# A fused linear-attention and feed-forward kernel: the last tiles written out engine by engine in another order, dead buffers for x1 and y, and Wq and Wk issued by SyncE

## The reference

```python
q = exp(split_heads(x @ Wq.T + bq)); k = exp(split_heads(x @ Wk.T + bk)); v = split_heads(x @ Wv.T + bv)
num = einsum(q, cumsum(k[..., :, None] * v[..., None, :]))
den = sum(q * cumsum(k))
x1  = layernorm(x + merge_heads(num / den) @ Wo.T + bo)
out = layernorm(x1 + tanh(x1 @ weight @ aux_weight1 @ aux_weight2 + bias))
```

## Time and profile before

| | us |
|---|---|
| median of 3 runs | 2287.44 (2287.05 to 2289.54) |
| the profiled execution | 2287.53 |
| its span | 2285.8 |
| mean granted clock of TensorE | 0.996 |
| PE busy | 2239.1 (98%) |
| DVE busy | 1546.1 (68%) |
| POOL busy | 1250.8 (55%) |
| ACT busy | 1014.6 (44%) |

### The profile page before, as it was taken

The page is one execution under the profiler, slowest core; times in us unless marked ns, Lnnn a source line. Parts: engine busy times, 40 slices in busy tenths (PEclk is TensorE's granted clock), DMA queues, the critical chain, the costliest instruction groups (busy, mean ns, idle before and its releaser), DMA issues.

```text
span 2285.8 us, 77469 instructions
## 1 busy us (share of the span) xinstructions
PE 2239.1 (98%) x27848; PEld 1829.1 (80%) x27848; DVE 1546.1 (68%) x2456; ACT 1014.6 (44%) x1695; POOL 1250.8 (55%) x1797
## 2 busy tenths in 40 slices
PE   7999999999999999999999999999999999999996
PEld 5778888888888888888888888888888888878874
DVE  4566766776776776676676677677677667667675
ACT  4344444444444444444444444444444444444443
POOL 2355555555555555555555555555555555555554
PEclk9999999999999999999999999999999999999999
DMA  8233333333333333333333333333333333333221
GB/s 179 65 100 106 116 106 103 116 108 103 113 111 102 110 114 100 108 118 102 107 116 104 105 116 106 103 116 108 103 112 112 99 112 114 102 105 116 70 75 47
DMA packets 292414, 241.60 MB, mean 106 GB/s; under 512 B 33184, under 2 KB 224160, under 8 KB 292128
## 3 DMA queue, kind: packets, MB, share of 16 engines
q1 hardware_dynamic: 290976, 235.02, 33.2%
q10 hardware_dynamic: 1152, 2.10, 0.4%
HBM read 139.20 MB, written 97.78 MB: 104 GB/s over the span
## 4 chain that ended last, share of the span: by engine, by line
PE 95%; DVE 1%; issue 1%; ACT 1%; POOL 1%; DMA 1%; SPq 0%; POOLq 0%; ACTq 0%; DVEq 0%
PE SC L339 26%; PE SC L341 25%; PE SC L340 25%; PE SC L430 6%; PE ND L406 6%; PE ND L397 3%; PE ND L393 2%; PE ND L441 2%; DMA WK<-a 1%; DVE o L828 0%; SPq L261 0%; POOL oL L958 0%; ACT A L661 0%; PE ND L339 0%; PE ND L341 0%
## 5 line engine op out<-in xcount | busy, mean ns | idle before, releaser
L940 POOL TENSOR_SCALAR_AFFINE_SELECT A<-A 128x512 f32<-128x512 f32 x512 | 329.7, 676 | 384.2 <-ACT A L661 384.1
L835 DVE TENSOR_TENSOR WK<-SC,bfbc 128x512 f32<-128x512 f32 x128 | 88.6, 692 | 623.1 <-PE SC L341 623.1
L828 DVE RECIPROCAL o<-ND 128x512 f32<-128x512 f32 x128 | 427.7, 3342 | 6.3 <-POOL oL L958 6.3
L952 POOL TENSOR_TENSOR x1L<-WK,x1H 128x512 fp32r<-128x512 f32 x125 | 161.6, 1293 | 469.7 <-ACT x1H L674 469.7
L661 ACT ACTIVATE A<-SC 128x512 f32<-128x512 f32 x512 | 264.6, 603 | 101.9 <-PE SC L430 101.9
L674 ACT ACTIVATE x1H<-WK 128x512 fp32r<-128x512 f32 x125 | 79.1, 633 | 334.4 <-DVE WK L872 334.4
L688 ACT ACTIVATE WK<-xres,shift,rstd 128x512 f32<-128x512 f32 x128 | 104.3, 815 | 276.5 <-POOL shift L968 276.5
L841 DVE TENSOR_TENSOR_SCAN WK<-ones,k,KT 128x128 f32<-128x128 f32 x512 | 207.3, 468 | 14.8 <-PE ND L393 14.8
L339 PE MATMUL SC<-xTH,WqH 128*128 128x512 f32 x512 | 209.4, 409 | 1.0 <-ACT A L661 1.0
L629 ACT ACTIVATE QT<-SC,bcol 128x512 f32<-128x512 f32 x128 | 88.3, 690 | 269.5 <-PE SC L341 269.5
L339 PE MATMUL SC<-WfH,x1H 128*128 128x512 f32 x512 | 199.7, 390 | 7.4 <-ACT x1H L672 3.0
(11 more groups left out here) (110 smaller groups left out, 5008.1 us busy)
## 6 DMA issues: line engine op xcount, KB each, us to landing
xres<-x SPq DMA_DIRECT2D x128, 256.0 KB, 2.7
out<-WK SPq DMA_DIRECT2D x128, 256.0 KB, 3.1
xin<-x SPq DMA_DIRECT2D x504, 64.0 KB, 1.9
x_rows<-WK SPq DMA_DIRECT2D x125, 256.0 KB, 2.0
WK<-x_rows SPq DMA_DIRECT2D x500, 64.0 KB, 2.1
k_rows<-WK SPq DMA_DIRECT2D x120, 256.0 KB, 2.1
WK<-k_rows SPq DMA_DIRECT2D x480, 64.0 KB, 1.9
A<-a1T SPq DMA_DIRECT2D x4, 256.0 KB, 6.2
```

The costliest lines, as they stand in the source:

```text
L828: nc.vector.reciprocal(o[:, :, :], den_ps).then_inc(recip_ready, 1)
L835: nc.vector.tensor_tensor(yf, ffn_ps, bfbc[:, :], ALU.add).then_inc(z_ready, 1)
L940: last = nc.gpsimd.affine_select(out=A[:, k % 2, j, :, :], in_=A[:, k % 2, j, :, :], compare_op=ALU.is_ge, fill=0.0, base=0, pattern=[[0, ...
L952: nc.gpsimd.tensor_tensor(halves[1], x1s[:, :].rearrange("p (t g q) -> p g t q", t=HG, q=HD), halves[0].bitcast(F32), ALU.subtract).then_i ...
```

## The change: what it does

The loop of the kernel is not touched but for the same code being put into named helpers. Two things change.

At the end, run_slots stops earlier (PE after slot 126, DVE after 126, ACT and POOL after 127), and each engine gets an `end()` with its remaining stages in an order of its own. Tiles 126 and 127 (`at_end`) write x1 to WK 4 and 5 and y to WK 6 and 7, and tile 126 uses oH and oL for the halves of x1. The turns of x1 are taken out of `feed_forward`.

At the start, SP issues the loads of Wq and Wk behind tile 3 and ahead of the biases; ACT issues no DMA any more.

```diff
@@ helpers
+        def x1_of(c, n):
+            return WK[:, 4 + n % 2, :] if c.at_end(n) else x1[:, n % 2, :]
+        def y_of(c, n):
+            return WK[:, 6 + n % 2, :] if c.at_end(n) else y[:, n % 2, :]
+        def x1_halves(c, n):
+            return (oH, oL) if c.at_end(n) and not c.at_end(n - 1) else (x1H, x1L)
@@ SyncE
             load_x(first, 3)
+            load_blocks(sp, wq_raw, wqT, wq_loaded)
+            load_blocks(sp, wk_raw, wkT, wk_loaded)
             load_biases()
@@ TensorE
+            def turn_x1(c, n):
+                pe.wait_ge(identity_ready, 1)
+                pe.wait_ge(scores_out[1], NT)
+                wait(pe, x1h_ready, c.count(n))
+                wait(pe, x1l_ready, c.count(n))
+                wait(pe, x1_ready, c.count(n + 1))
...
+            def end():
+                first_half(*place(NT - 1))
+                output_projection(*place(NT - 3))
+                denominators(*place(NT - 1))
+                attend(*place(NT - 1))
+                output_projection(*place(NT - 2))
+                feed_forward(*place(NT - 4))
+                turn_x1(*place(NT - 3))
+                output_projection(*place(NT - 1))
+                turn_x1(*place(NT - 2))
+                feed_forward(*place(NT - 3))
+                turn_x1(*place(NT - 1))
+                feed_forward(*place(NT - 2))
+                feed_forward(*place(NT - 1))
@@ ScalarE
+            def write_x1(c, n):
+                wait(act, shift1_ready, c.count(n + 1))
+                if not c.at_end(n):
+                    wait(act, y_ready, c.count(n - 1))
...
+            def end():
+                split_o(*place(NT - 1))
+                tanh(*place(NT - 4))
+                split_turned_x1(*place(NT - 3))
+                write_x1(*place(NT - 2))
+                split_turned_x1(*place(NT - 2))
+                write_out(*place(NT - 4))
+                write_x1(*place(NT - 1))
+                split_turned_x1(*place(NT - 1))
+                tanh(*place(NT - 3))
+                write_out(*place(NT - 3))
+                tanh(*place(NT - 2))
+                tanh(*place(NT - 1))
+                write_out(*place(NT - 2))
+                write_out(*place(NT - 1))
             split_aux(0)
-            load_blocks(act, wq_raw, wqT, wq_loaded)
             split_aux(1)
-            load_blocks(act, wk_raw, wkT, wk_loaded)
@@ VectorE
+            def end():
+                sum_ffn(*place(NT - 5))
+                prefix_sums(*place(NT - 1))
+                normalise(*place(NT - 2))
+                add_bias(*place(NT - 3))
+                turn_x1(*place(NT - 4))
+                statistics(*place(NT - 5))
+                residual(*place(NT - 3))
+                add_bias(*place(NT - 2))
+                normalise(*place(NT - 1))
+                residual(*place(NT - 2))
+                sum_ffn(*place(NT - 4))
+                rest_of_turned_x1(*place(NT - 3))
+                add_bias(*place(NT - 1))
+                statistics(*place(NT - 4))
+                residual(*place(NT - 1))
+                rest_of_turned_x1(*place(NT - 2))
+                sum_ffn(*place(NT - 3))
+                rest_of_turned_x1(*place(NT - 1))
+                statistics(*place(NT - 3))
+                sum_ffn(*place(NT - 2))
+                sum_ffn(*place(NT - 1))
+                statistics(*place(NT - 2))
+                statistics(*place(NT - 1))
@@ GpSimd
+            def end():
+                rest_of_o(*place(NT - 1))
+                scale_x1(*place(NT - 2))
+                add_x1(*place(NT - 4))
+                scale_out(*place(NT - 4))
+                scale_x1(*place(NT - 1))
+                add_x1(*place(NT - 3))
+                scale_out(*place(NT - 3))
+                add_x1(*place(NT - 2))
+                add_x1(*place(NT - 1))
+                scale_out(*place(NT - 2))
+                scale_out(*place(NT - 1))
```

More of the change, by code:

```diff
@@ L575, in _ @@
             second_half(*place(NT - 2 * B))
-            for t in range(NT - 2 * B + 1, NT + 3):
+            for t in range(NT - 2 * B + 1, NT - 1):
                 first_half(*place(t))
                 second_half(*place(t))
+            end()
         @block.scalar
@@ new lines, in split_o @@
+            def split_o(c, n):
+                wait(act, o_ready, c.count(n + 1))
+                wait(act, oproj_done, c.count(n))
+                nc.scalar.activation(oH[:, :, :], o[:, :, :], ACT.Copy).then_inc(oh_ready, 1)
+            def write_x1(c, n):
+                wait(act, shift1_ready, c.count(n + 1))
+                if not c.at_end(n):
+                    wait(act, y_ready, c.count(n - 1))
+                nc.scalar.activation(x1_of(c, n), xres[:, n % 2, :], ACT.Identity, bias=shift[:, 0:1],
+                                     scale=rstd[:, 0:1]).then_inc(x1_ready, 1)
@@ L648, in slot, with tanh, write_out @@
+            def tanh(c, n):
+                wait(act, z_ready, c.count(n + 1))
+                nc.scalar.activation(y_of(c, n), y_of(c, n), ACT.Tanh).then_inc(tanh_ready, 1)
+            def write_out(c, n):
+                wait(act, shift2_ready, c.count(n + 1))
+                nc.scalar.activation(y_of(c, n), y_of(c, n), ACT.Identity, bias=shift[:, 1:2],
+                                     scale=rstd[:, 1:2]).then_inc(out_ready, 1)
             def slot(c, k):
-                att = c.exists(k)
@@ L650, in slot @@
                 proj = c.exists(k + 4)
[L651 to L662, removed]
+                if c.exists(k - 4):
+                    tanh(c, k - 4)
@@ L663, in slot @@
+                keep_scores(c, k)
                 if proj:
                     keep_q(c, k)
-                if att and not proj:
+                else:
                     copy_v(c, k)
                 if c.exists(k - 3):
[L668 to L676, removed]
@@ new lines, in normalise, with add_bias @@
+            def normalise(c, n):
+                wait(dve, num_done, c.count(n + 1))
+                wait(dve, oh_ready, c.count(n))
+                wait(dve, ol_ready, c.count(n))
+                nc.vector.reciprocal(o[:, :, :], den_ps).then_inc(recip_ready, 1)
+                wait(dve, recip_ready, c.count(n + 1))
+                nc.vector.tensor_tensor(o[:, :, :], num_ps, o[:, :, :], ALU.mult).then_inc(o_ready, 1)
+            def add_bias(c, n):
+                wait(dve, xres_loaded[n % B], c.dma_count(n))
+                nc.vector.tensor_tensor(xres[:, n % 2, :], xres[:, n % 2, :], cbc[:, :], ALU.add).then_inc(xb_ready, 1)
@@ new lines, in slot @@
+                if c.exists(k - 1):
+                    normalise(c, k - 1)
+                if c.exists(k - 2):
+                    add_bias(c, k - 2)
+                if c.exists(k - 3):
+                    turn_x1(c, k - 3)
+                if c.exists(k - 2):
+                    residual(c, k - 2)
+                if c.exists(k - 4):
+                    statistics(c, k - 4)
+            def end():
[22 more added lines that the diff above has]
+                statistics(*place(NT - 1))
```

349 lines of the change are left out of this document (176 added, 173 removed).

## The result

The changed kernel takes 2276.09 us (median of 5 runs, 2274.22 to 2278.65), the kernel before in the same runs 2287.44: 11.35 us less; the ratio of the runs is 0.9947 (95% interval 0.9933 to 0.9962). Measured once more beside other kernels it came to 0.9945 (0.9931 to 0.9959). The forecast was 2275.8, with 2272.0 to 2280.8 as its range.

The account below looks back on a forecast made before the run. The loop was taken as bound by TensorE (PE), with time to be had only at the two ends: 8.3 us at the end plus 3.4 at the start, 11.7 off 2287.5, giving 2275.8 us, range 2272.0 to 2280.8.

Parts of the forecast that it names:

- tile 127's layer norm: At the end: residual 2255.3 to 2256.0, statistics 2257.0, POOL's operations 1.5 us, x1(127) written 2259.3 in old time.
- the two gaps: PE idle left at the end: 0.9 us before turn(127) and 1.6 us before ffn(127).
- The last chain: After the last matmul: sum, tanh, addition, statistics and output of tile 127, written 6.9 us behind it, before 6.1.
- gaps two and three: At the end: feed-forwards waiting for their own x1 turn's round trip, 1.49 to 1.69 us uncovered; spare halves shorten this.
- gap one: At the end: PE's 4.34 us idle before output product 126 goes, with its half-clock stretch of 1.6 us.
- the end's gain is halved: Rival, 8%: fixed order on POOL and ACT makes engines wait for each other; 8.3 falls to 4, time 2280.1 us.
- block 3: At the start: aux block 3 lands at 14 to 15 us instead of 25.25; PE loses its 7.07 us gap.
- T: At the start: when Wk lands, forecast 25 us; w's split done T+12.7, 37.9, 5.2 us sooner.
- the half clock: At the start: after PE's short gaps, 8 matmuls at 0.43 us spacing instead of 0.23, costing 1.6 us.
- the rival that I gave 20%: At the start: no slow clock, Wk landing at 24 to 25 us, time 2273.0 to 2274.2 us; chance 20%.
- The 0.2 us for the biases: At the start: a loss of 0.2 us because the biases now land behind Wk.
- SP's eight added issues: At the start: some 0.43 us each; cost nil while the queue has a backlog, 3.4 us at most if not.

Follow-up runs that it names:

- gap_one: Kernel before with output product 125 ahead of the last attention on PE and normalise(127) behind residual(125) on DVE, no spare buffers; median 2284.39 us, ratio 0.9980.
- one_pair: Changed kernel without the spare pair of x1 halves: tile 126's go to x1H and x1L again, waiting for feed-forward 125; ratio 0.9981 to the kernel before.
- w_first: Changed kernel with w's 1 MB load moved ahead of Wq and Wk on SP; ratio 0.9955 to the kernel before.
- act_late: Changed kernel with the Wq and Wk loads back on ACT, but issued after its split of aux block 2; 2275.67 us, ratio 0.9946 to the kernel before.
- end_more: Changed kernel with the last feed-forward in the values' PSUM bank, tanh(126) ahead of output 125, last addition on DVE; ratio 0.9931 to the kernel before.
- start_only: Kernel before with only the Wq and Wk loads moved to SP, the end left alone; median 2285.46 us, ratio 0.9983.
- end_only: Changed kernel with Wq and Wk issued by ACT again as before; median 2281.60 us, ratio 0.9969 to the kernel before.

## Why the prediction was right

**The end (8.3 forecast, 7.6 measured).** Step by step it went as worked out. With 5.05 us taken off for the earlier arrival, I had product 126 at 2240.4 (2240.35), the turn of 125 at 2246.0 (2245.97), turn(126) at 2249.7 (2249.93). The step that was mis-sized is tile 127's layer norm: the write of x1(127), forecast to start at 2253.4, started at 2254.00. Its bias took 1.23 us instead of 0.68, while POOL's addition for tile 124 ran:

```profile
2248.18 1.29 POOL L1051 TENSOR_TENSOR WK<-WK 128x512 f32<-128x512 f32 x1
```

From there all is 0.5 to 0.7 late, and the two gaps are 1.01 and 1.37 where I had 0.9 and 1.6. The last chain is 6.96 us, forecast 6.9.

The shares were less well told than the sum. I put gaps two and three beside gap one; gap_one shows that 5.6 us come from the moves of gap one alone, output product 125 ahead of the last attention and residual(125) ahead of normalise(127). The two were not tried apart. And the rival "the end's gain is halved", an engine waiting in a fixed order, did not happen here, but one_pair shows that it was one buffer away, and dearer (6.3 us) than the 4.3 at which I priced it, because of the clock.

**The start (3.4 forecast, 5.45 measured).** The mechanism was right: block 3 at 15, Wk at 25.12 against T = 25, product at T + 12.6 against T + 12.7. That T was met to 0.1 us is partly luck, since it varied from 24.35 to 26.66 with the same loads. T + 12.4 to 12.8 held in the six further profiles with this order, over a T from 24.70 to 28.41. Of the 5.45 us, 4.39 are the sooner T (29.51 to 25.12) and 1.06 the shorter way behind it (13.66 to 12.60), which is about what DVE no longer loses beside POOL on the first Wk block (1.77 to 0.69 us). The term that was wrong is the half clock, 1.6 us, that I took for PE's short gaps by the nearest row, 1.84 us. The gaps came as 1.41, 1.47, 0.62 and 1.61 us, without the 2.7 that I had among them, and none was followed by it, nor was the gap before the product in any of the other profiles (1.61 to 1.64 us). Even where the half clock came, in w_first behind a gap of 4.24 us, the product still began at T + 12.43, after 1.64 us of idle: on the way to the product it is DVE that ends last, not PE. So the case that came true at the start is the rival that I gave 20%, the start with all of its gain. The 0.2 us for the biases were not seen either. SP's eight added issues (12.14 to 15.89 us) cost nothing that shows: in act_late, where ACT issued these loads, T and the product were no sooner (25.59 and 38.01). By the Trainium skill, DMA: Bandwidth & Descriptors, section Rules for kernel authors, which says that spreading loads over engines saves only the time of issuing them, I had read that the start would gain nothing. The trace agrees with the rule (217 GB/s from 20 to 25 us against 220) and not with that reading of it: the order of the bytes gave 5.45 us.

**The sum.** Ends of -5.45 and -7.62, the middle +0.40, the store -0.13: 12.8 us of span. 11.7 had been forecast. That the sum was met so closely is luck in part: the start was 2.05 us better than forecast, the end 0.7 worse, the middle, put at nothing, 0.4 longer, and so only 1.0 us is left between 2275.8 and the profiled 2274.8. The median, 2276.09, lies closer still, because the profiled execution was among the faster of its five. The ends of the stated range, 2272.0 and 2280.8, are a little off their own sums (2287.5 less 6.2 and 8.8 is 2272.5, less 6.5 is 2281.0), which changes nothing here.

**Left open.** The middle, whose code for PE is the same in all kernels, was 2194.3 to 2195.0 us in the three profiles with the old start, and 2194.7 to 2196.5 in the nine with a sooner weight product, 1.1 us more on average. act_late (2195.74) speaks against SP as the issuer as its cause. The traces say where it arises: not behind the start. PE begins the same small product of an early slot at 225.94 us in the kernel before, 225.98 in end_only, 220.47 in the changed kernel and 222.16 in start_only, which is 182.71 to 182.77 us behind the weight product in all four. The difference gathers later, in a few single pauses of 0.2 to 0.8 us in the loop and behind it, most of them at other places in other profiles. In some PE waited for ACT's keys, in others for nothing that the profile shows. The longest in start_only (timeline of PE) is of the second kind; the kernel before ran through there:

```profile
2106.92 0.44 PE L443 MATMUL ND<-V,WK 128*32 128x32 f32 x29
2108.00 0.25 PE L443 MATMUL ND<-V,WK 128*32 128x32 f32 x3 [0.64 <-issue]
```

So the sooner start arrives whole in the loop. Whether the pauses are chance or a price of it stays open: one near 2050 us (0.2 to 0.8 us longer than in the others) stands in seven of the nine profiles with the sooner product and in none of the three with the old start. If they are a price, the start nets some 4.4 us instead of 5.45. The ratios of end_only and the changed kernel, 0.9969 and 0.9947, lie 5.0 us apart, those of the kernel before and start_only 3.9, and do not decide it.

## What to carry to other kernels

Where the bound engine runs dry at the end, look for the one long operation that stands ahead of a short one which the bound engine needs; moving it can bring most of what a rewritten order brings. A load that is issued from a second queue is not free for the first: put what is needed later behind what is needed first, on whichever queue. Price a gap of the bound engine with the clock that follows it, and look at what is queued behind each added wait before giving up a spare buffer.

## What the runs showed of the hardware

The cost of a gap on TensorE was uneven. After 1.0 to 1.8 us of idle at either end of the changed kernels, after 2.24 us in one_pair and after 2.61 us at the end of gap_one, the spacing stayed at 0.23 us. After 4.34 us it was 0.43, for seven matmuls in the kernel before, ten in one_pair and all twelve in start_only; between the first and the last the same code differs by 0.9 us. The length of the gap alone does not decide: at the old start, where gaps of 7.07 and 4.95 us had gone before, 1.84 us in the kernel before and 2.42 in end_only were followed by 0.43 us spacing too. And the half clock can come late: in end_only after two matmuls at full clock, and in w_first, where PE had idled 4.24 us at the start, after three. PE's timeline there:

```profile
25.34 0.47 PE L355 MATMUL SC<-xTH,WqH 128*128 128x512 f32 x1 [4.24 <-DVE WqL L822]
25.65 0.40 PE L356 MATMUL SC<-xTL,WqH 128*128 128x512 f32 x1
25.88 0.41 PE L357 MATMUL SC<-xTH,WqL 128*128 128x512 f32 x1
26.12 0.61 PE L355 MATMUL SC<-xTH,WqH 128*128 128x512 f32 x1
26.52 0.63 PE L356 MATMUL SC<-xTL,WqH 128*128 128x512 f32 x1
```

There it did not move the weight product, as told above.

VectorE's addition of two SBUF operands took 1.23 us beside an addition on GpSimd that was under way, 0.68 alone, and ended 0.55 us behind it (2250.02, 2249.47). The same 0.55 us stand behind GpSimd's end in three more such cases: another bias of the changed kernel (0.99 us, 2240.80 behind 2240.25), its low part of an aux block (1.37 us, 17.01 behind 16.46), and the first Wk block of the kernel before (1.77 us, 32.09 behind 31.54). So what VectorE loses is the rest of GpSimd's operation. The Trainium skill, SBUF — State Buffer, section Who interferes with whom, says that such an operation and a GpSimd operation that reads SBUF exclude each other, the second waiting for the first; the trace agrees.
